# Decoder layer in fp32 on one core: the q, k and v projections as three F32R products of split halves

## What is computed

```python
def _L0_attn_ref(x, W, b):                       # x: layer norm of the input
    qkv = jnp.einsum('btc,oc->bto', x, W) + b    # C = 256, W is 768 x 256
    q, k, v = jnp.split(qkv, 3, axis=-1)         # 16 heads of 16
    att = jnp.einsum('bhtd,bhsd->bhts', q, k) / math.sqrt(D)
    att = jax.nn.softmax(jnp.where(causal, att, -jnp.inf), axis=-1)
    y = jnp.einsum('bhts,bhsd->bhtd', att, v)
x = x + _L0_attn_ref(_layernorm(x), ...)
x = x + _L0_xattn_ref(_layernorm(x), ctx_1024, ...)
x = x + _L0_ffn_ref(_layernorm(x), ...)
```

## Time and profile before

| | |
|---|---|
| median of 3 runs | 3295.55 us (3292.09 to 3298.89) |
| the profiled execution | 3280.96 us, its span 3279.1 us |
| TensorE busy | 3058.4 us (93%), 26632 instructions |
| its weight loads | 2417.7 us (74%) |
| VectorE busy | 2565.8 us (78%) |
| ScalarE, GpSimd busy | 1753.8 us (53%), 1272.7 us (39%) |
| DMA, mean | 110 GB/s |

### The profile page before, as it was taken

The page is one execution under the profiler, slowest core; times in us unless marked ns, Lnnn a source line. Parts: engine busy times, 40 slices in busy tenths (PEclk is TensorE's granted clock), DMA queues, the critical chain, the costliest instruction groups (busy, mean ns, idle before and its releaser), DMA issues.

```text
span 3279.1 us, 78416 instructions
## 1 busy us (share of the span) xinstructions
PE 3058.4 (93%) x26632; PEld 2417.7 (74%) x26632; DVE 2565.8 (78%) x6882; ACT 1753.8 (53%) x3260; POOL 1272.7 (39%) x1773
## 2 busy tenths in 40 slices
PE   3899999999999999999999999999849999999998
PEld 2677777777777777777777777777539999999997
DVE  2687888788788888878888887888638888888886
ACT  1465555556555655555565565556424545454543
POOL 3233333333333333333333343333214545455554
PEclk8999999999999999999999999999869999999999
DMA  5665556556556655655565565566233333434341
GB/s 100 88 110 111 98 109 115 104 99 113 112 96 111 112 103 103 112 106 98 111 112 104 102 115 107 99 107 107 56 110 136 128 138 128 142 123 146 122 149 47
DMA packets 321569, 359.70 MB, mean 110 GB/s; under 512 B 62040, under 2 KB 289631, under 8 KB 321248
## 3 DMA queue, kind: packets, MB, share of 16 engines
q1 hardware_dynamic: 308384, 321.96, 47.8%
q0 software_dynamic: 12864, 33.64, 3.1%
HBM read 140.93 MB, written 46.21 MB: 57 GB/s over the span
## 4 chain that ended last, share of the span: by engine, by line
PE 85%; DVE 8%; issue 4%; DMA 1%; SPq 1%; POOL 0%; ACT 0%; DVEq 0%; POOLq 0%
PE psum L624 15%; PE psum L986 12%; PE psum L970 12%; PE psum L619 8%; PE psum L723 4%; PE psum L811 4%; PE psum L701 3%; PE psum L710 3%; PE psum L677 3%; PE psum L674 3%; PE psum L789 3%; PE psum L668 3%; DVE negmax L1207 2%; PE psum L803 2%; PE psum L827 2%
## 5 line engine op out<-in xcount | busy, mean ns | idle before, releaser
L1039 ACT ACTIVATE PA<-psum 128x512 f32<-128x512 f32 x512 | 305.9, 598 | 354.6 <-PE psum L710 350.5
L1207 DVE TENSOR_REDUCE negmax<-psum 128x2 f32<-128x512 f32 x512 | 344.2, 683 | 106.8 <-PE psum L677 99.7
L1144 ACT ACTIVATE hT_high<-psum,b_sb 128x512 fp32r<-128x512 f32 x280 | 193.2, 690 | 415.2 <-PE psum L970 393.2
L1045 ACT ACTIVATE PC<-psum 120x512 f32<-120x512 f32 x512 | 303.8, 596 | 206.4 <-PE psum L803 205.6
L1204 DVE TENSOR_REDUCE negmax<-psum 128x4 f32<-128x512 f32 x256 | 177.0, 691 | 250.0 <-PE psum L677 243.8
L1212 DVE TENSOR_REDUCE cnegmax<-psum 128x4 f32<-128x480 f32 x512 | 324.5, 644 | 7.6 <-PE psum L789 7.4
L986 PE MATMUL psum<-wo_high,hT_low 128*128 128x256 f32 x1120 | 319.8, 286 | 0.6 <-DVE hT_low L1488 0.6
L986 PE MATMUL psum<-wo_low,hT_high 128*128 128x256 f32 x1120 | 316.9, 283 | 0.0
L986 PE MATMUL psum<-wo_high,hT_high 128*128 128x256 f32 x1120 | 316.9, 283 | 0.0
L1488 DVE TENSOR_TENSOR hT_low<-hT,hT_high 128x512 fp32r<-128x512 f32 x280 | 267.0, 972 | 52.4 <-ACT hT L1145 52.4
L624 PE MATMUL psum<-zT,wqk_sb 128*128 128x256 f32 x1024 | 266.3, 383 | 2.9 <-DVE q_rest L1230 2.2
(11 more groups left out here) (211 smaller groups left out, 8255.3 us busy)
## 6 DMA issues: line engine op xcount, KB each, us to landing
QP<-q_parts SPq DMA_DIRECT2D x384, 128.0 KB
KP<-k_parts SPq DMA_DIRECT2D x384, 128.0 KB, 4.2
QC<-cq_parts SPq DMA_DIRECT2D x384, 128.0 KB, 3.9
w_high<-w_high_dram SPq DMA_DIRECT2D x35, 1024.0 KB, 5.1
w_low<-w_low_dram SPq DMA_DIRECT2D x35, 1024.0 KB, 7.0
fx<-rows_dram SPq DMA_DIRECT2D x35, 514.0 KB
x_in<-in_x SPq DMA_DIRECT2D x64, 256.0 KB, 4.7
x_res<-in_x SPq DMA_DIRECT2D x64, 256.0 KB, 5.1
```

The costliest lines, as they stand in the source:

```text
L1039: act.activation(dst, psum[:, ST_BANKS[n % 2], :], ACT.Exp, scale=D ** -0.5).then_inc(exp_done.sem, 1)
L1045: act.activation(PC[0:M, 2 * n:2 * n + 2, :].rearrange("p h n -> p (h n)"), psum[0:M, ST_BANKS[n % 2], :], ACT.Exp, scale=D ** -0.5).then_ ...
L1144: act.activation(hT_high[:, m, :], psum[:, m % 4, :], ACT.Gelu, bias=b1_sb[:, q, m:m + 1])
L1207: dve.tensor_reduce(negmax[:, 1, h:h + 2], bank.rearrange("p (h k) -> p h k", h=2), AX_X, ALU.max).then_inc(max_done.sem, 1)
```

## The change

The rows and the weights of the projections are each cut in a high half, rounded to F32R, and a low half, the rest, also F32R. Each fp32 product becomes three F32R products: high weight by low rows, low by high, high by high, in the order that the code gives, accumulated in the same PSUM block. ScalarE's copy of the turned rows writes `zT_high` in place of `zT`, in the same slot. VectorE gets a subtract of 128x512, PSUM less `zT_high`, in slot 13, behind max 5; `project_q` waits for it. Before the loop ScalarE makes one more copy, and VectorE five subtracts, for the weights' halves; the first products wait for these.

```diff
+            def project_split(bank, lhs, rhs, width, m):
+                products = [(a, z) for kc in range(KC) for a, z in ((lhs(kc, m)[1], rhs(kc)[0]), (lhs(kc, m)[0], rhs(kc)[1]), (lhs(kc, m)[0], rhs(kc)[0]))]
+                for n, (a, z) in enumerate(products):
+                    last = pe.matmul(psum[:, bank, m * width:(m + 1) * width], a, z, start=(n == 0), stop=(n == len(products) - 1))
+                return last
+            def w_halves(kc, cols):
+                return wqk_high[:, kc, cols], wqk_low[:, kc, cols]
+            def z_halves(kc, rows=slice(0, T)):
+                return zT_high[:, kc, rows], zT_low[:, kc, rows]
...
             def project_q(b, m):
                 if m == 0:
-                    pe.wait_ge(zT_copied.sem, zT_copied.value(b))
-                last = project(7, lambda kc, m: wqk_sb[:, kc, m * P:(m + 1) * P], lambda kc: zT[:, kc, :], T, m)
+                    pe.wait_ge(zT_low_made.sem, zT_low_made.value(b))
+                last = project_split(7, lambda kc, m: w_halves(kc, slice(m * P, (m + 1) * P)), z_halves, T, m)
...
             def project_k(b, m):
...
-                last = project(7, lambda kc, m: wqk_sb[:, kc, C + m * P:C + (m + 1) * P], lambda kc: zT[:, kc, :], T, m)
+                last = project_split(7, lambda kc, m: w_halves(kc, slice(C + m * P, C + (m + 1) * P)), z_halves, T, m)
...
             def project_v(i):
...
-                    last = project(6, lambda kc, m: zT[:, kc, m * P:(m + 1) * P], lambda kc: wv_sb[:, kc, :], C, t)
+                    last = project_split(6, lambda kc, m: z_halves(kc, slice(m * P, (m + 1) * P)), lambda kc: (wv_high[:, kc, :], wv_low[:, kc, :]), C, t)
...
-            pe.wait_ge(wqk_by_dim, 2 * KC)
+            pe.wait_ge(wqkv_low_made, 2 * KC + 1)
...
                     if n == 12 and runs(i, -1):
-                        copy_z(i + 1, xT_made, v_made, zT, 7, zT_copied)
+                        copy_z(i + 1, xT_made, v_made, zT_high, 7, zT_copied)
...
+            copy(wv_high[:], wv_in).then_inc(wqk_by_dim, 1)
             steps(act, body)
...
+            def subtract_high_z(b):
+                dve.wait_ge(zT_copied.sem, zT_copied.value(b))
+                dve.tensor_tensor(zT_low[:].rearrange("p c n -> p (c n)"), psum[:, 7, :], zT_high[:].rearrange("p c n -> p (c n)"), ALU.subtract).then_inc(zT_low_made.sem, 1)
...
+                    if n == 13 and runs(i, -1):
+                        subtract_high_z(i + 1)
...
+            for kc in range(KC):
+                for w in range(2):
+                    dve.wait_ge(wqk_by_dim, 2 * kc + w + 1)
+                    dve.tensor_tensor(wqk_low[:, kc, w * C:(w + 1) * C].rearrange("p (c d h) -> p c d h", c=KC, d=D),
+                                      wqk_in[:, kc, w * C:(w + 1) * C].rearrange("p (h c d) -> p c d h", c=KC, d=D),
+                                      wqk_high[:, kc, w * C:(w + 1) * C].rearrange("p (c d h) -> p c d h", c=KC, d=D), ALU.subtract).then_inc(wqkv_low_made, 1)
+            dve.wait_ge(wqk_by_dim, 2 * KC + 1)
+            dve.tensor_tensor(wv_low[:], wv_in, wv_high[:], ALU.subtract).then_inc(wqkv_low_made, 1)
             steps(dve, body)
```

More of the change, by code:

```diff
@@ L108, in decoder_kernel @@
         minus_half = sb("minus_half", [P, TS])
-        wqk_sb = sb("wqk_sb", [P, KC, 2 * C])
-        wv_sb = sb("wv_sb", [P, KC, C])
+        wqk_high = sb("wqk_high", [P, KC, 2 * C], F32R)
+        wqk_low = sb("wqk_low", [P, KC, 2 * C], F32R)
+        wv_high = sb("wv_high", [P, KC, C], F32R)
+        wv_low = sb("wv_low", [P, KC, C], F32R)
         bqk_sb = sb("bqk_sb", [P, 2 * KC])
@@ L150, in decoder_kernel @@
         z = during_attention("z", [P, NT, C])
-        zT = during_attention("zT", [P, KC, T])
+        zT_high = during_attention("zT_high", [P, KC, T], F32R)
+        zT_low = during_attention("zT_low", [P, KC, T], F32R)
         q_parts = during_attention("q_parts", [P, 3, KC * T], BF16)
@@ L221, in decoder_kernel @@
         wqk_in = PA[:].rearrange("p h n -> p (h n)")[:, 0:KC * 2 * C].rearrange("p (c n) -> p c n", c=KC)
+        wv_in = PA[:].rearrange("p h n -> p (h n)")[:, KC * 2 * C:KC * 3 * C].rearrange("p (c n) -> p c n", c=KC)
         wq_in = PC[:].rearrange("p h n -> p (h n)")[:, 0:KC * C].rearrange("p (c n) -> p c n", c=KC)
@@ L300, in decoder_kernel @@
         wqk_by_dim = semaphore("wqk_by_dim")
+        wqkv_low_made = semaphore("wqkv_low_made")
         wq_by_dim = semaphore("wq_by_dim")
@@ L335, in decoder_kernel @@
         zT_copied = signal("zT_copied", 1)
+        zT_low_made = signal("zT_low_made", 1)
         q_high = signal("q_high", 1)
@@ L427, in _ @@
                 (wqk_in, wqkvT[:, 0:2 * C].rearrange("(c p) n -> p c n", p=P)),
-                (wv_sb[:], wqkvT[:, 2 * C:3 * C].rearrange("(c p) n -> p c n", p=P)),
+                (wv_in, wqkvT[:, 2 * C:3 * C].rearrange("(c p) n -> p c n", p=P)),
                 (bv_sb[:], bv.broadcast_to([P, C])),
@@ L1121, in _ @@
                 for w in range(2):
-                    copy(wqk_sb[:, kc, w * C:(w + 1) * C].rearrange("p (c d h) -> p c d h", c=KC, d=D),
+                    copy(wqk_high[:, kc, w * C:(w + 1) * C].rearrange("p (c d h) -> p c d h", c=KC, d=D),
                          wqk_in[:, kc, w * C:(w + 1) * C].rearrange("p (h c d) -> p c d h", c=KC, d=D)).then_inc(wqk_by_dim, 1)
+            copy(wv_high[:], wv_in).then_inc(wqk_by_dim, 1)
             steps(act, body)
```

## The result

The changed kernel took 3299.16 us (median; 3292.82 to 3308.27) and the kernel before, run beside it, 3291.47 us (3287.32 to 3298.89): a ratio of 1.0019, 95% interval 1.0011 to 1.0027. The change makes the kernel 7.7 us slower. The forecast was 3307 us, +11.8 us on the profiled execution. Of the 8.2 us between 3307.4 and 3299.2, 4.1 come from the starting point (the three executions shown before have a median of 3295.55, the twenty beside the change, which include these three, 3291.47) and 4.1 from the step itself, 7.7 us in place of 11.8.

A forecast was written before the change was run, and what follows sets the result against it. Each attention turn was taken as bound by the k operand up to slot 8, TensorE to slot 18, then VectorE. 59 turns x 0.20 = +11.8 us on 3280.96 gave 3292.8, on the median's scale 3307; range 3279 to 3323.

The forecast's parts named there:

- the starting point: Scale of the forecast time: median of the runs shown, 3295.55 us, 14.6 above the profiled execution; it gave 3307.
- part 1: Turn_max to slot 8, set by the k operand: v's 0.29 us worth nothing, k_mid's earlier start taken as 0.
- TensorE's part: Projections: each call 0.15 us shorter, 0.87 us a turn; only q's 0.29 us counts, v's and k's go into waits.
- part 2: Slot 8 to slot 18, where TensorE is dense: it grows by 0.19 to 0.27 us a turn.
- VectorE's part: Subtract in slot 13, taken as 0.60 us, delays the rz rows; their transposes start 0.28 to 0.36 us later.
- The refund: The rz instructions, moved behind GpSimd's w_rest, take 0.73 instead of 0.90 us: 0.17 us back.
- rival C: Dearer: no refund, or moved operations meet others; 0.37 to 0.45 us a turn, +25 us, 3320; chance 0.16.
- Rival F: Full port hold at rz: refund 0.43 us in all, part 2 changes by -0.07 a turn, 3291; chance 0.02.
- rival B: Late rz rows, but k_mid's 0.24 us a turn is passed on to slot 8: -2 us, 3293; chance 0.20.
- my row at 528 us: Turn with late cz, where GpSimd's subtract took 1.32 us and ended 1.03 after cz; basis for taking k_mid's gain as 0.
- Head: Before the loop and its first turns: up to 4 us of added work against up to 4 us gained; put at 0.
- A: The forecast itself: the rz rows come late, 0.14 to 0.27 us a turn, 3304 to 3312; chance 0.43.

The follow-up runs named there:

- e6: Kernel before, with ScalarE's k_mid moved ahead of slot 3's exponential: 3285.19 against 3293.88 us, 0.9977.
- e7: Changed kernel with q and k as fp32 products of the high halves, v alone by split products, no subtract: 3290.39 against 3293.88 us, 0.9994.
- e15: Kernel before, unedited, run again for a second profile: 3290.38 us.
- e16: Kernel before, unedited, run again for a third profile: 3290.62 us.
- e11: Changed kernel itself, run again beside e12 on the same chip: 3300.57 against 3292.45 us, 1.0024.
- e3: Changed kernel with v by fp32 products of the high halves alone: 3294.14 against 3292.87 us, 1.0000.
- e12: The same kernel as e3, run beside e11: 3298.61 us, 1.0024 of the kernel before.
- e2: Changed kernel without VectorE's subtract, the rows' high halves standing in for the low ones: 3279.07 against 3292.87 us, 0.9953.
- e4: Changed kernel with the rz rows' transposes (and their copy) moved behind the second q call: 3279.13 us, 0.9961 of the kernel before.
- e10: Changed kernel with the load of x_in moved behind the transfers of k's parts: 3247.57 against 3292.45 us, 0.9867.
- e5: Kernel before, with the load of x_in moved behind the transfers of k's parts: 3242.68 against 3293.88 us, 0.9846.
- e13: Changed kernel with two useless matmuls filling TensorE's wait at slot 8: 3297.22 against 3289.94 us, 1.0022.
- e14: Kernel before, with the same two useless matmuls in slot 8 as e13: 3285.87 us, 0.9988.
- e1: Kernel before plus VectorE's new subtract alone, result unused, project_q waiting for it: 3310.31 against 3292.87 us, 1.0049.
- e8: Changed kernel with the edits of e4 and e5 together: 3224.79 us, 0.9794 of the kernel before.

## Why the prediction came out as it did

The 59 turns from the fifth turn_max to the last, in us, with 1.66 taken off for each fall of the clock, make the traces comparable (e6 and e7 are there for what is said of part 1):

| | loop | falls | loop less falls | fifth turn_max |
|---|---|---|---|---|
| before | 2111.68 | 0 | 2111.7 | 201.57 |
| e15, before | 2120.06 | 5 | 2111.8 | 202.96 |
| e16, before | 2115.95 | 2 | 2112.6 | 203.95 |
| changed | 2131.07 | 3 | 2126.1 | 200.29 |
| e11, changed | 2132.06 | 4 | 2125.4 | 200.50 |
| e3, v in fp32 | 2120.29 | 1 | 2118.6 | 199.38 |
| e12, v in fp32 | 2129.33 | 4 | 2122.7 | 198.94 |
| e6, k_mid first | 2115.06 | 0 | 2115.1 | 202.70 |
| e7, v split alone | 2117.04 | 0 | 2117.0 | 200.95 |

The loop less falls grew by 2125.7 - 2112.0 = 13.7 us, 0.23 a turn.

The mechanism came out as forecast. Two steps of the sum had the wrong size, and one reason was wrong although its result was right:
- *"On its scale 3307"*, the starting point: 4.1 us too high.
- *"59 x 0.20 = +11.8 us"*, taken from one profile to medians: the traces bear it out (+11.3), the medians gave +7.7. Some 2.5 of the 4.1 us between them go with the granted clock, about which the sum said nothing; the rest is open.
- *Part 1*: "its end hangs on cz, which doesn't move". It doesn't hang on cz in the changed kernel.

In detail:

- **TensorE's part: right.** A call of project_split is 0.72 us. v and k gave nothing (e7, the waits on V, slot 8 and next_row); q's two calls shorten part 2 once nothing stalls behind them (0.22 us a turn in e2, 0.31 in e4), though part 1 then takes 0.14 and 0.21 back.
- **VectorE's part: right to 0.02 us.** Forecast: rz's transposes 0.28 to 0.36 later, 0.06 for the exposed load, 0.15 back; part 2 grows by 0.19 to 0.27. Measured: +0.27 to the transposes' start and -0.08 from there to the logits (0.06 less 0.15), +0.19 a turn, 11.2 us in all. The refund came as said: rz takes 0.73 instead of 0.90, so rival C, which denies it, fell. Rival F, which more than doubles it, had its sum wrong from the start: of a pair that took 0.90 us with a neighbour and 0.73 without, no hold can give back more than 0.17.
- **Part 1: right in its result, wrong in its reason.** I wrote that GpSimd's subtract would be held by cz and end as before. It starts 0.24 us earlier and isn't held: in 46 of 57 turns VectorE pays (cz 1.67 us), and GpSimd's subtract ends 0.15 us before cz. By my own sign (an end under 1.03 us after cz) that spoke for rival B, whose gain then didn't come.
- **Part 1, where the reason failed: the choice of the row.** In my row at 528 us GpSimd's subtract started 0.43 us after cz; the forecast's own times put it 1208.05 - 1207.69 = 0.36 us after, and that is the other side of a border. In the 18 traces together it starts up to 0.36 us after cz in 550 turns, and in every one of them VectorE's pair takes 1.61 to 1.67 us and GpSimd keeps its 1.16. It starts 0.38 us after or later, while the second cz instruction is under way, in 81 turns, and in every one the pair keeps its 0.73 us and GpSimd's subtract ends 1.02 us after it. The six turns in between go either way.
- **The port.** By the Trainium skill, "SBUF — State Buffer", section "Who interferes with whom", a VectorE instruction in one of its two-port modes and GpSimd share one pair of ports, and whoever issues first holds the pair for the whole instruction while the other blocks. The 631 turns on either side of the border agree with it; the mode of cz isn't in the trace. The hold is also as long as that rule says: the second cz instruction ends 0.15 us behind GpSimd's subtract, and in the kernel before the first rz instruction ended 0.15 us behind w_rest (1228.89 against 1228.74), with 0.58 us in place of 0.40. My reckoning of a full hold (rz's end at 1229.47) let the whole 0.73 us begin when the hold ended; the records show that only 0.15 us of the held instruction is left then.
- **Part 1, why no gain.** The result, no gain, still came out, for a reason that I had not given: the DMA engines are 93 to 94% busy up to slot 8, and k's last transfer, issued 0.15 us earlier, lands no earlier. Rival B needed the 0.24 to pass. Slot 8 comes 12.35 us after turn_max in the three profiles of before and 12.40 in the two of the changed kernel: 59 x 0.05 = +3 us instead of B's -14. So the early subtract rather costs a little than gains: the loops of e3 and e12, which keep k_mid and v as before, are 3 to 7 us shorter than the changed kernel's, and those of e6 and e7, which start the subtract early, 3 and 5 us longer than before's. TensorE's wait for V (14.4 us) isn't the whole reason, since in e6 it is only 2.0 us and slot 8 still comes at 12.40. The cause of these 3 us was not found.
- **Head: inside its 4 us.** The fifth turn_max comes 2.4 us earlier (200.4 against 202.8, means; the three of before differ by as much). The gain lies between the first turn_max and the fifth, where the turns have no rz rows, as the forecast had it.
- **The sum: right by the traces, too large for the medians.** 13.7 - 2.4 = +11.3 us by the traces; the profiled executions differ by 3301.8 - 3290.5 = 11.3 (changed kernel and e11, with 7 falls together, against e15 and e16, also with 7). The forecast's +11.8 is that. But the medians gave +7.7 and +8.1 in the plain pair, where the intervals reach from 4 to 11 us, +4.9 to +6.3 in e10 over e5, and +11.35 in e13 over e14, where the profiles show no fall of the clock.
- **The clock, the part that the sum left out.** Every execution on record has its mean granted clock beside its time. Over 90 executions of the kernel before it is 0.9772, over 32 of the changed kernel (its own 20 and e11's 12) 0.9783. The traces show the clock at two levels alone, full and half. So that is an estimate of 150 and 143.5 us at the lower one (2 x (1 - clock) x time). In the 90 executions each us more at the lower level goes with 0.39 us more time (correlation 0.80). So the 6.5 us are worth some 2.5 us, and the means, 3292.2 and 3299.4 us, would differ by 9.7 instead of 7.2 at an equal clock. The other edited kernels lie on the same side: 0.9787 in e1, 0.9788 in e2, 0.9789 in e7, 0.9792 in e3 and e6, 0.9796 in e13 and 0.9800 in e14; only e4, with 0.9772, doesn't. Why the changed kernel is granted a little more is open (its two profiles have as many falls in the loop as e15 and e16), and so are the 1.6 us that are left, which is less than the scatter between sets (e3, e12).
- **The starting point: the other half of the miss.** I took the three times shown as the scale. Their median was 4.1 us above that of the later twenty, and the profile that carried the sum was 10 us below its usual execution. It is faster than every one of the 110 executions of this kernel beside the changed one and the experiments (the fastest took 3283.62 us), and its granted clock of 0.981 stands for 126 us at the lower level where the mean is 150: 24 x 0.39 = 9 of the 10 us, by the estimate above. What the sum rests on (0.19 a turn) was untouched, since falls and landings are in neither term.
- **Forecast and range.** The sign was that of A. 1.0019 lies just inside the 0.2% that I set as the border of "same", and 3299.2 just under A's own range (3300 to 3314): for a step of 12 us and a starting point known to 4, that range was too narrow.

What stays open as well: e6's -8 us. Its loop, without a fall, is 2115.06 us, 3 longer than that of before less falls. Its mean granted clock of 0.9792 stands for 136 us at the lower level against 150, which is worth some 5 of the 8 us. No run shows what grants it more.

## What to carry to other kernels

An engine that is 93% busy and 85% of the chain can give up 29 us while the kernel gets slower: ask for every piece of the gain what is late behind it, and for every new instruction on another engine who is queued behind that. Moving one stage of a few tenths of a us behind its neighbour turned a loss of 8 us into a gain of 14 (e4): before paying for an operation with a wait, look for independent work to put in front of the waiting one. Where the wait is on transfers and the DMA engines are over 90% busy, look at the order of the queue before the arithmetic: one load put behind k's transfers brought 51 us, more than six times what the change cost. Before a row is used as a model for another turn, compare the order of starts to a few hundredths of a us: 0.43 and 0.36 us after cz were two different cases. And a sum read from one profile belongs to the granted clock of that one execution.

## What the runs showed of the hardware

- In some turns TensorE's granted clock fell to 1.2 GHz for about 3.4 us, costing 1.56 to 1.66 us each. A wait of 1.88 to 2.29 us stood behind every fall seen in the loop, but waits up to 2.35 us (e4) also passed without one. With two fillers (0.43 us together) in the wait (e13, e14) there was none, nor with the wait itself shorter (e5, e8, e10). That the fillers did it is likely and not shown: the first profile of the kernel before, with five waits of 1.88 us or more, and e6, with four, had none either.
- Two VectorE instructions in sequence (cz, SBUF to SBUF, 0.73 us together) and a GpSimd subtract (1.16 us, both inputs in SBUF) hold each other up by the order of their starts. Where the subtract starts up to 0.36 us after the first, the pair takes 1.61 to 1.67 us and the subtract its 1.16 (550 of 550 turns); where it starts 0.38 us after or later, inside the second, the pair keeps its 0.73 and the subtract takes up to 1.37 (81 of 81). A held VectorE instruction ended 0.15 us behind the GpSimd one (cz, and rz behind w_rest).
- With the DMA engines 93 to 94% busy, a transfer issued 0.15 us earlier landed 0.08 us later; one load of 256 KB taken from ahead of it brought its landing from 12.26 to 11.63 us after turn_max.
- A single profile of this kernel can lie 10 us under its median, with 126 us at the lower clock where the mean is 150.
